# Decoder layer on one core: routing groups 1 and 2 of the experts moved forward, norms of the last two batches split between GpSimd and VectorE

## What is computed

```
x: (4, 256, 256); every line is done per batch of 256 tokens, 4 batches, 8 tiles of 128 tokens
y   = attention(layernorm(x)) @ Wout.T          # causal, 16 heads of 16, rotary positions
x   = x + y
adj = (1-g) * layernorm(x) + g * (A + A.T) / 2  # A = sigmoid(sim) where sim is among its row's 76 largest
x   = x + adj                                   # sim = Q K.T from ctx_512, g = sigmoid(gamma_raw)
h   = layernorm(x)
s   = sigmoid(h @ gate_w)                       # 64 experts in 8 groups of 8
best 4 groups by the sum of their two largest (s + bias), best 6 experts in them
x   = x + 2.5 * sum(weight * expert(h)) + shared_expert(h)   # at most 48 tokens per expert
```

## Time and profile before

| what | value |
|---|---|
| median of 3 runs | 301.23 us (300.86 to 301.93) |
| span of the profiled execution | 299.4 us, 5226 instructions |
| mean granted TensorE clock | 0.897 |
| busy: PE, DVE, POOL, ACT | 76%, 69%, 45%, 32% |
| HBM traffic over the span | 194 GB/s |

### The profile page before, as it was taken

One profiled execution on the slowest core, in us unless ns is written; L12 is line 12 of the kernel. 1 busy time (PEld: TensorE's weight loads), 2 busy tenths in 40 slices (PEclk: granted clock), 3 DMA queues, 4 the chain that ended last, 5 costly groups with the idle time before them and its releaser, 6 DMA issues.

```text
span 299.4 us, 5226 instructions
## 1 busy us (share of the span) xinstructions
PE 226.2 (76%) x1836; PEld 165.8 (55%) x1836; DVE 207.2 (69%) x668; ACT 95.6 (32%) x154; POOL 134.1 (45%) x182
## 2 busy tenths in 40 slices
PE   8883586598889888879566214494989999896993
PEld 3672475486678577659335103243457766653882
DVE  3699999979989998987692671912145334751697
ACT  1444530522434555566154014010013333333000
POOL 2810767616115300236677757777204655673000
PEclk9999589599999999999978755588699999999899
DMA  6608979694085999923208999990599999921996
GB/s 213 195 0 108 106 110 168 95 124 87 0 107 78 305 398 382 350 72 134 93 27 259 283 283 298 300 244 14 107 200 211 255 262 217 279 83 41 378 387 198
DMA packets 36890, 55.78 MB, mean 186 GB/s; under 512 B 6556, under 2 KB 26790, under 8 KB 36864
## 3 DMA queue, kind: packets, MB, share of 16 engines
q1 hardware_dynamic: 31680, 47.75, 62.6%
q10 hardware_dynamic: 768, 3.54, 5.7%
q0 software_dynamic: 4416, 4.15, 4.8%
HBM read 32.93 MB, written 25.17 MB: 194 GB/s over the span
## 4 chain that ended last, share of the span: by engine, by line
POOL 18%; PE 15%; issue 11%; DVE 10%; DMA 6%; another core or an unknown queue 4%; ACT 2%; ACTq 0%; POOLq 0%; SPq 0%; DVEq 0%
POOL slot_rows L996 15%; PE unit L644 5%; PE proj L663 3%; DMA arena<-expert_rows 2%; DVE arena L1432 2%; DMA arena<-slot_rows 2%; PE unit L630 2%; DVE arena L1168 2%; PE outp L653 1%; DVE arena L1434 1%; POOL rstd L897 1%; DVE arena L1438 1%; DMA slot_rows<-rows,arena 1%; DVE arena L1436 1%
## 5 line engine op out<-in xcount | busy, mean ns | idle before, releaser
L996 POOL DMA_INDIRECT slot_rows<-rows,arena x48 | 47.6, 992 | 23.9 <-issue 12.1
L1018 POOL DMA_INDIRECT expert_rows<-arena x28 | 28.3, 1010 | 34.0 <-ACT arena L870 27.5
L805 ACT ACTIVATE arena<-unit 128x1024 f32<-128x1024 f32 x24 | 24.6, 1024 | 42.8 <-PE unit L488 37.4
L1168 DVE TENSOR_REDUCE arena<-unit 128x4 f32<-128x1024 f32 (+1 forms) x24 | 28.9, 1212 | 3.1 <-PE unit L475 3.1
L1057 DVE MAX8 arena<-arena 128x8 f32<-128x256 f32 x80 | 30.6, 414 | 0.3
L488 PE MATMUL unit<-arena 128*128 128x256 bf16 (+1 forms) x128 | 29.2, 248 | 0.0
L1062 DVE MATCH_REPLACE8 arena<-arena 128x256 f32<-128x256 f32 x72 | 29.0, 409 | 0.0
L487 PE MATMUL unit<-arena,identb 128*128 128x128 bf16 x128 | 25.8, 222 | 0.0
L895 POOL TENSOR_SCALAR nmean<-mv 128x2 f32<-128x2 f32 x12 | 2.8, 236 | 46.0 <-DVE mv L1095 41.4
L486 PE MATMUL unit<-arena 96*128 96x128 bf16 (+1 forms) x96 | 22.3, 253 | 0.6 <-ACT arena L805 0.6
L475 PE MATMUL unit<-arena,identb 128*128 128x128 bf16 x128 | 20.8, 227 | 0.0
(11 more groups left out here) (221 smaller groups left out, 550.9 us busy)
## 6 DMA issues: line engine op xcount, KB each, us to landing
ring<-in_w_gu SPq DMA_DIRECT2D x16, 384.0 KB
expert_rows<-blank SPq DMA_DIRECT2D x8, 768.0 KB, 9.5
arena<-in_w_gu SPq DMA_DIRECT2D x16, 384.0 KB, 13.3
arena<-expert_rows SPq DMA_DIRECT2D x7, 768.0 KB, 9.2
slot_rows<-blank SPq DMA_DIRECT2D x1, 4608.0 KB, 17.3
arena<-slot_rows ACTq DMA_DIRECT2D x12, 288.0 KB
arena<-ring_dn SPq DMA_DIRECT2D x24, 128.0 KB, 4.5
ring_dn<-in_w_dn SPq DMA_DIRECT2D x16, 192.0 KB
```

The costliest lines, as they stand in the source:

```text
L805: act_fn(prob[:, n, :], unit_at((key, b)), ACT.Exp, scale=D ** -0.5).then_inc(unit_free((key, b)), 1)
L996: pool.indirect_dma_start(out=slot_dram, out_offset=bass.IndirectOffsetOnAxis(ap=place[:, t, k:k + 1], axis=0), in_=rows[:, t, :], in_offs ...
L1018: pool.indirect_dma_start(out=z_dram, out_offset=bass.IndirectOffsetOnAxis(ap=rowi[:, p:p + 1], axis=0), in_=yrow[:, p % NY, :], in_offset ...
L1168: v.tensor_reduce(nmax[:, t, c * u:c * u + c], unit_at((key, b)).rearrange("p (h k) -> p h k", k=n), axis=AX, op=ALU.max, negate=True).the ...
```

## The change

- STEPS is rewritten from D1c1 on. The row above it is kept. Group 0's 25 steps to `sel_ready` (now 14, below) stand in one block ahead of U13, its last 12 ahead of U23; group 1's stand in two blocks behind D1e2; group 2's selection stands ahead of D1e3 (the last attention residual), the rest behind it. 9 filler steps more stand ahead of MS3.
- For groups 0 and 1 the 12 DVE steps of the group sums go. POOL makes them in `group_sums` (H0, H1): s + bias twice side by side, then four additions of the vector to itself shifted by 1 to 4, and DVE takes one maximum over the 32 pair sums of each group. The penalty and its addition (L1264, L1267) become one instruction for each tile, for all groups.
- For batches 2 and 3 POOL makes only the power of layernorms 2 and 3. The addition of epsilon, the scaling and the shift go to DVE, and so does x3 (two TENSOR_SCALARs, from ACT). The mixing is split: DVE scales the rows by itself, ACT scales the adjacency earlier (stage Y), DVE adds.
- The last residual goes tile by tile from proj; the logits of batches 2 and 3 go through outp, the transposed adjacency of batch 3 and the counts of group 2 through unit.
- The three memsets ahead of the last stores move to DVE, behind its routing. The first 12 stores no longer wait for score units.
- Weights of pairs 2 to 12 and 14 to 21 are loaded once the last `pv` and the adjacency are done, that of pair 13 after the last projection. PE's warm-up stands ahead of two waits instead of behind them.

```
@@ STEPS
-    D1d0 U12 A2d3 D1e0 U22 F5 U32 D20 U42 F1 D1a2 U52 F1 MS2 V0 F1 ME2 MT3 D1b1 F5 D1c1 D3a0 F6 D3b0 G9 U03 D1d1 G7 U13
-    F1 D1e1 G7 U23 G4 U33 D21 U43 Z2 F1 G5 Z1 G2 P0 U53 MS3 G5 D3a1 ME3 MT4 D1b2 F4 D3b1 Z3 D1c2 R1 G1 U04 F3 G13 Z1 D1d2
-    F1 Z3 U14 G2 U24 F3 D1e2 Z3 G16 U34 G5 F5 P1 U44 D22 U54 ME4 D1b3 G5 D1a3 Z1 D3a2 F1 D1c3 Z5 G5 D1d3 F2 Z4 F1 G2 D1e3
-    F1 Z2 F1 D3b2 G1 R2 Z1 G48 F1 D23 Z1 P2 Z5 D3a3 F1 D3b3 Z4 F1 R3 MS4 G1
+    D1d0 U12 A2d3 D1e0 U22 F5 U32 D20 U42 F1 D1a2 U52 F1 MS2 V0 F1 ME2 MT3 D1b1 F5 D1c1 N0 D3a0 F6 D3b0 H0 F4 U03 D1d1 G14 U13
+    F1 D1e1 P0 G4 F1 G8 Z2 U23 F3 U33 D21 Z6 F1 U43 F1 U53 MS3 N1 D3a1 ME3 F1 MT4 D1b2 F2 D3b1 H1 Z2 D1c2 D1d2 F6 U04 D1e2 Z2
+    R1 G14 U14 Y2 U24 P1 G12 U34 U44 D22 U54 F4 ME4 N2 D3a2 D1b3 D1c3 D1a3 D1d3 Z12 D3b2 Y3 R2 G25 D1e3 P2 G12 Z2 D23 N3
+    D3a3 D3b3 R3 MS4
...
@@ sync
-                if (stage, b) == ("D3a", 1):
-                    filled(sp, "unit", (T_UNITS[-1], 2))
+                if (stage, b) == ("D1b", 3):
+                    filled(sp, "out", (1, 3))
                     sp.wait_ge(adj_row, B)
+                    fills(*range(RA - 6, RA + 5), *range(RA + 6, RP))
+                if (stage, b) == ("D1e", 3):
+                    filled(sp, "proj", ("att", B - 1))
+                    fills(RA + 5)
...
@@ tensor
+            pe.wait_ge(placed[KE - 3], 16 * NT)
+            keep_clock(WARM, outp)
             emptied(pe, "unit", ("sd", 0))
             emptied(pe, "unit", ("sg", 1))
-            pe.wait_ge(placed[KE - 3], 16 * NT)
-            keep_clock(WARM, outp)
...
@@ scalar
+            def mixing_scaled(b):
+                if b >= LATE:
...
+                    for t in range(TPB):
+                        act_fn(mix[:, t, :], adj[:, TPB * b + t, :], ACT.Copy, scale=gam[:, 3:4]).then_inc(mix_scaled, 1)
...
@@ gpsimd, inverse_root
+                if kind != "ln1" and b >= LATE:
+                    late = n - NORMS.index(("ln2", LATE))
+                    gp.wait_ge(var_late, late + 1)
...
+                    pool.tensor_tensor(rstd[:, k, :], srs[:, :], cexp[:, 0:1].broadcast_to((P, TPB)), ALU.pow).then_inc(root_ready, 1)
+                    return
...
+            def group_sums(n):
+
+                ts = slice(TPB * n, TPB * n + TPB)
+                emptied(gp, *LOGITS[n])
+                if n >= 1:
+                    gp.wait_ge(place_ready, n)
+                g8 = score[:, ts].rearrange("p t (g j) -> p t g j", g=NG)
+                b8 = biasb[:, :].rearrange("p (g j) -> p g j", g=NG).unsqueeze(1).broadcast_to((P, TPB, NG, NE // NG))
+                pool.tensor_tensor(twice[:, :, :, 0:8], g8, b8, ALU.add)
+                link(pool.tensor_tensor(twice[:, :, :, 8:12], g8[:, :, :, 0:4], b8[:, :, :, 0:4], ALU.add))
+                for k in range(4):
+                    end = pool.tensor_tensor(pairs[:, :, :, k, :], twice[:, :, :, 0:8], twice[:, :, :, k + 1:k + 9], ALU.add)
+                end.then_inc(group_ready, 1)
...
@@ place_rows
-                    if done < TPB * KE and done % 2 == 0 and 0 <= done // 2 - 1 < len(T_UNITS) - 1:
-                        filled(gp, "unit", (T_UNITS[done // 2 - 1], B - 1))
...
@@ end of the stores
-            place_rows(NT * KE - TPB * KE - (NT * KE - len(placements)))
-            gp.wait_ge(x3_ready, B)
-            filled(gp, "gen", ("att", B - 1))
-            link(pool.memset(xgT, 0.0))
-            link(pool.memset(rowi, FAR))
-            pool.memset(wslot, 0.0).then_inc(moe_pads, 1)
-            place_rows(TPB * KE)
+            place_rows(len(placements))
...
@@ vector
+            def inverse_root(kind, b):
...
+                ve.wait_ge(root_ready, n + 1)
...
+                if kind == "ln2":
+                    need(mark(v.tensor_scalar(rstd[:, k, :], rstd[:, k, :], gam[:, 2:3], None, ALU.mult)))
+                    mark(v.tensor_scalar(grow[:, :], rstd[:, k, :], 1.0, None, ALU.add))
+                v.scalar_tensor_tensor(shift[:, k, :], mv[:, k, :, 0], -1.0, rstd[:, k, :], ALU.mult, ALU.mult).then_inc(norm_late, 1)
+                normed(ve, kind, b)
...
+                    for t in range(TPB):
+                        r = res[:, TPB * b + t, :]
+                        ends.append(mark(v.tensor_scalar(r, r, grow[:, t:t + 1], shift[:, 1, t:t + 1], ALU.mult, ALU.add)))
+                    for t in range(TPB):
+                        r = res[:, TPB * b + t, :]
+                        ve.wait_ge(mix_scaled, TPB * (b - LATE) + t + 1)
+                        need(ends[t])
+                        end = mark(v.tensor_tensor(r, r, mix[:, t, :], ALU.add))
...
+            def moe_input(b):
+                if b < LATE:
+                    return
+                inverse_root("ln3", b)
                 for t in range(TPB):
...
+                    ins = v.tensor_scalar(x3[:, TPB * b + t, :], res[:, TPB * b + t, :], rstd[:, 2, t:t + 1], shift[:, 2, t:t + 1], ALU.mult, ALU.add)
...
@@ routing
+                if n < LATE:
+                    ve.wait_ge(group_ready, n + 1)
+                    biased = twice[:, :, :, 0:8]
+                    done = mark(v.tensor_reduce(gsum[:, ts, 0:NG], pairs.rearrange("p t g k j -> p t g (k j)"), axis=AX, op=ALU.max))
                     yield
...
+            x3_made(ve, B - 1)
+            v.memset(xgT, 0.0)
+            v.memset(rowi, FAR)
+            v.memset(wslot, 0.0).then_inc(moe_pads, 1)
```

More of the change, by code:

```diff
@@ L91 @@
 AREAS["proj"] += [("sd", 1)]
+LOGITS = [("out" if ("D3b", n) in BESIDE else "gen", ("lg", n)) for n in range(B)]
 def nth(area, name):
@@ L357, in stack, with fills @@
                             sp.dma_start(to, src).then_inc(stack_in[b], 16)
-            later = {("A2d", 1): range(0, 1), ("A2d", 2): range(1, RA - 6), ("D3a", 1): range(RA - 6, RA + 5), ("D3a", 3): range(RA + 5, RP)}
+            def fills(*pairs):
+                for p in pairs:
+                    ring_fill(p)
             for stage, b in STEPS:
@@ new lines, in mixing @@
+            def mixing(b):
+                if b >= LATE:
+                    inverse_root("ln2", b)
+                normed(ve, "ln2", b)
+                if b < LATE:
+                    ve.wait_ge(spread_ready, b + 1)
+                    for t in range(TPB):
+                        r = res[:, TPB * b + t, :]
+                        end = mark(v.scalar_tensor_tensor(r, r, grow[:, t:t + 1], mix[:, t, :], ALU.mult, ALU.add))
+                    need(end)
+                else:
+                    ends = []
+                    for t in range(TPB):
+                        r = res[:, TPB * b + t, :]
+                        ends.append(mark(v.tensor_scalar(r, r, grow[:, t:t + 1], shift[:, 1, t:t + 1], ALU.mult, ALU.add)))
+                    for t in range(TPB):
+                        r = res[:, TPB * b + t, :]
+                        ve.wait_ge(mix_scaled, TPB * (b - LATE) + t + 1)
+                        need(ends[t])
+                        end = mark(v.tensor_tensor(r, r, mix[:, t, :], ALU.add))
+                    need(end)
+                stats("ln3", b, rows_of(b))
+                if b >= LATE:
+                    variance_shifted("ln3", b)
@@ L1376, in _ @@
                    "MT": shifts_turned, "MS": shift_parts, "D1a": add_transposed, "D1c": head_average, "D1e": attention_residual,
-                   "D2": mixing, "R": route_next, **{f"U{n}": maxima(n) for n in range(6)}}
+                   "D2": mixing, "N": moe_input, "R": route_next, **{f"U{n}": maxima(n) for n in range(6)}}
             for stage, b in STEPS:
```

232 lines of the change are left out of this document (152 added, 80 removed).

## The result

The changed kernel took 316.03 us (median of 4 runs, 313.51 to 317.18), the kernel before 301.05 in runs beside it: ratio 1.050, 95% interval 1.042 to 1.057. It is slower by 5%, and outside the predicted range. The profiled execution of the changed kernel has a span of 315.0 us.

The account below looks back on a forecast made before the run. Bound: POOL's 48 stores and batch 3's data chain, meeting at 195, then a fixed tail. The last store moves 2.3 us earlier: 299.4 - 2.3 = 297.1 of span, 298.9 us with 1.8 around it; range 295.3 to 302.3.

Parts of the forecast that it names:

- Group 0: Group 0's routing: six POOL additions some 2.9 us; places at about 125 against 132.5, first store 7 us earlier.
- What pays for it: 9 more filler steps ahead of MS3, 3.3 us: next score stage 3 to 5 us later.
- the shift of the score units is smaller: Rival, chance 0.16: MS3 1 us late, not 4; group 3's places at 189.6, 296 us.
- Group 1: Group 1's routing: D1e2 at 144.7 without the 3.55 us hole, `sel_ready` at 150.5 against 148.2, stores from 158 to 173.3.
- the hole comes back: Rival, chance 0.15: the 3.55 us hole before D1e2 recurs in batch 3's score units; 302.4 us.
- Group 2: Group 2's routing: R2 starts at 164.3 against 167.98; places at 174.9 against 176.38.
- The norms: Norms of the last sequence, POOL keeping only a 0.72 us power: x3 ready at 180.3 against 181.78, 1.5 gained.
- Group 3: Last routing: places at 192.6, last 12 stores from 192.9 against 195.23, last store at 206.9 against 209.28: 2.3 us gained.
- The credit of 2.1 us: Gain forecast in the data chain: group 3's places at 192.6 against 194.74 before.
- Costed at nothing: Weights, memsets on DVE, shared expert's products, sigmoid's table load and dropped score-unit waits were taken to cost the end nothing.
- The rule against the change: DVE TENSOR_SCALARs and POOL stores block each other at SBUF ports; as a rival up to 2 us later, 300.9, chance 0.10.
- The rival itself: The rival that the 3.55 us hole before D1e2 recurs: 302.4 us, chance 0.15.

Follow-up runs that it names:

- e5: Changed kernel, two GpSimd sums in place of each store but a token tile's first choice (40 of 48 stores left out): 296.92 us, ratio 0.995.
- e16: Kernel before, two GpSimd sums in place of each store but a tile's first choice (40 of 48 left out): 298.55 us, ratio 0.985.
- e15: Changed kernel, norms of sequences 2 and 3 made as in the kernel before: 315.33 us, ratio 1.040.
- e10: Kernel before, two GpSimd sums (1.2 us) behind every second one of the first 24 stores: 311.25 us, ratio 1.031.
- e18: Changed kernel, one 128x256 GpSimd sum behind every second of the first 24 stores, SP issuing both halves of the first four slot reads: 299.31 us, ratio 0.986.
- e9: Changed kernel, two GpSimd sums behind every second of the first 24 stores, shared_out(1) moved behind the warm-up products: 307.06 us, ratio 1.014.
- e1: Changed kernel, SP issuing the eight transfers that zero expert_rows only once group 0's places are ready: 313.7 us, ratio 1.039.
- e4: Changed kernel, zeroing of expert_rows once group 0's places are ready and weight fills as in the kernel before: 312.73 us, no ratio.

## Why the prediction was wrong

What the stores cost, from the times of group 3's places:

| stores | before | changed |
|---|---|---|
| all 48 | 194.7 | 206.1 |
| sums for 40 of them | 193.0 | 193.0 |
| 8 only | 186.2 | 188.6 |
| 1st less 2nd | 1.7 | 13.1 |
| 2nd less 3rd | 6.8 | 4.4 |

The fourth row is the least that late signals cost. The fifth is not the price of an occupied GpSimd alone: the sums also lengthen DVE's instructions, and between the places of group 1 and of group 3 DVE is busy for 4.6 us longer in e5 than in the changed kernel, which is as much as the whole 4.4. So late signals make the places of group 3 some 13 to 17.5 us later in the changed kernel (206.1 less 193.0, and less 188.6). A pair of sums is also 0.2 us shorter than a store.

- *Group 0*: right. Places at 124.0 (forecast 125), the first store at 124.88. The six additions took 2.3 us in the trace, from 112.19 to 114.51 (0.45, 0.32 and 1.51 for four), and not 2.9.
- *What pays for it*: overestimated. MS3 came 1.5 us later (132.78 against 131.26) and not 3 to 5. This was the condition of the rival *the shift of the score units is smaller*, and its gain was lost in the next hole.
- *Group 1, the first step that failed.* It had D1e2 at 144.7 and `sel_ready` at 150.5; they came at 149.87 and 155.1. The 3.55 us hole was taken to be absent in the likeliest case, and it came back as 5.8 us at 139.86. That was the rival *the hole comes back*, priced as one hole. Behind the hole TensorE ran slower: its granted clock was 0.54 from 140 to 150, and the projection (L608) that D1e2 waits for took 3.27 us, with 1.89 for that of batch 2 before. In e5, without the hole, the clock was 1.00 from 140 to 148 and D1e2 started at 141.15. So D1e2 came 8.7 us later than without the hole of 5.8, and the sum, which carried PE's durations over, had no term for it.
- *Group 2, the step that failed most.* R2 was to start at 164.3, and started at 179.96. The twelve stores of group 1 start at 162.09, 4 us later than forecast, as one row, while sequence 3's heads, transposes and logits pass between PE, ACT and DVE; five signals in a row come 2.0, 4.3, 5.3, 9.0 and 2.0 us late. The sum had made DVE's and PE's durations carry over and gave the stores no price but their own time on GpSimd. Without late signals (e5) the places of group 2 come at 173.0, and the sum had 174.9.
- *The norms* and *Group 3*: from places of group 2 to places of group 3 the sum had 17.7 us, the changed kernel took 17.0. Places of group 3 at 192.6 in the sum, 193.0 in e5. But that agreement is in part luck: e5 had group 2 at 173.0 and took 20.0 us from there, as its sums hold up DVE. What the sum says of a kernel whose signals come in time is not refuted, and not shown to a microsecond. The kernel before has 193.0 with sums as well (e16), and 186.2 against 188.6 with 8 stores, so that in neither pair the change wins anything in this chain. The credit of 2.1 us was against 194.7, of which late signals are at least 1.7.
- *Costed at nothing*: the tail. PE's signals under the last twelve stores came 7.7 and 10.2 us late (shared_in(1) ended at 212.65 and shared_out(0) at 214.38, DVE adds the latter at 224.60), so the second silu ran at 220.33, shared_out(1) at 221.79, for 3.75 us at a granted clock of 0.50 (shared_out(0), the same products, took 1.89 at 212.49 and a clock of 1.00), and the warm-up products behind it. The expert products start 10.9 us after the last store, 8.7 before: 2.3 of the 4.4 us. The other 2.1 lie in the expert phase (granted clock 0.96 there, 0.98 before), and no run was made for them.
- *The rule against the change*, of shared SBUF ports: it isn't what made the holes, as they are gone in e5, where GpSimd's sums read and write SBUF beside the same DVE instructions. It does act between sums and DVE (1.64 us for a pair of TENSOR_SCALARs). Beside stores it cost 0.19 us for a pair at most: 0.92 at 189.63 and 0.74 at 193.46, both beside stores, 0.73 at 158.48 beside none. The store of 1.24 us that the prediction took for a sign of it is the first store of each trace, in e5 too.
- *The rival itself*: right in its mechanism's place, wrong in its size (302.4) and so in its chance. Its reading "it was there once" missed what the trace of before already had: ACT's waits of 1.94 and 3.47 us for "remote" in the same row, and DVE's of 5.16 at 209.82. It took one hole as the unit; what recurred was the cause, in three rows of stores. Its own time, 302.4, lay just outside the range given, 302.3.

In short, the step that failed is the price of the stores: nothing but their own time on GpSimd, and one 3.55 us hole that was left out of the sum. The runs showed late signals worth 13 us or more at group 3's places.

Putting the norms back on GpSimd wins nothing (e15): one hole goes and a wait for GpSimd takes its place. Their move is what lets gaps help: in the kernel before the same gaps cost 3% (e10), since GpSimd's norm instructions are on its chain. Which part of the change brings the late signals stays open. Its order of steps puts group 1's twelve stores in one row under sequence 3's chain, but the kernel before has ten in a row there without a late signal, and the order wasn't undone by itself.

## What to carry to other kernels

A hole that the profile gives to "remote" or to an unknown queue is a price of something, and has to be tied to its cause before anything is moved near it: one run with sums in place of stores would have done that ahead of the change. Where a trace shows late signals in a row of indirect stores from GpSimd, try to break the row in pairs, with one sum of 0.63 us between them as in e18, and check who waits for GpSimd behind it: in the kernel before, gaps made it worse. A row as such is no proof of harm, so look at the signals under it first. A control that puts other work in place of an instruction has side effects of its own; look at the durations beside it. An engine that issues a load behind a wait on a late signal hands the delay on to the load.

## What the runs showed of the hardware

While GpSimd issues indirect stores one after another (0.97 us each, 1.28 apart), signals of finished TensorE work can reach DVE and ACT 2 to 10 us late, 12.3 in e9, where 0.03 to 0.04 us is usual. It takes some stores in a row: in the row of 131.33, signals of 134.0 are late by 0.8 and those of 134.8 and 135.8 by 3.7 and 4.1. It doesn't happen in every row: not in the kernel before at 158 to 171 and at 181 to 194, nor in e15 at 167 to 172. What tells the rows apart, no run here shows. It doesn't depend on the bytes written (1.61 or 4.15 MB, in 4416 packets both times), nor on other DMA traffic alone (e1, e4), and 0.6 us more between pairs of stores takes most of it away. Through what path a store holds up another engine's signal, no run here shows.

GpSimd's sums of 128x256 hold up DVE's TENSOR_SCALARs of 128x256: a pair of these took 1.64 us beside sums, 0.74 to 0.92 beside stores and 0.73 beside neither.
